# A transformer block on one core: the first norm moved to the token layout, and a new order of work on five engines

## The reference

```python
h = _layernorm(x) * (1 + ca) + sa                                # first norm
x = x + ga * _L0_attn_ref(h, Wqkv, bqkv, Wout, bout, rel_emb)    # 16 heads of 8, relative bias, softmax
h = _layernorm(x) * (1 + cb) + sb                                # second norm
x = x + gb * _L0_ffn_ref(h, ...)                                 # router, 16 experts, top 4
# second block, its own modulations
h = _layernorm(x) * (1 + ca) + sa                                # third norm
x = x + ga * _L1_attn_ref(h, Wk, Wv, Wo, gate, freqs)            # running sums of v * rotor, and of v * conj(k shifted)
h = _layernorm(x) * (1 + cb) + sb                                # fourth norm
x = x + gb * _L1_ffn_ref(h, W_r, W_k, W_v, mu_r, mu_k)           # mix with the token before, sigmoid, squared relu
```

## Time and profile before

| what | us |
|---|---|
| median of 3 runs | 1566.75 (1566.13 to 1572.26) |
| the profiled execution | 1568.34, its span 1566.6 |
| busy in the span: PE, DVE, ACT, POOL | 1409.5, 1180.5, 856.1, 304.8 |
| setup, to 47.7 | 47.7 |
| step 0, to 143 | 95.3 |
| a step of the loop | 90.5 |
| the last step, without an `a` | 65.6 |

### The profile page before, as it was taken

The page is one execution under the profiler, slowest core; times in us unless marked ns, Lnnn a source line. Parts: engine busy times, 40 slices in busy tenths (PEclk is TensorE's granted clock), DMA queues, the critical chain, the costliest instruction groups (busy, mean ns, idle before and its releaser), DMA issues.

```text
span 1566.6 us, 23671 instructions
## 1 busy us (share of the span) xinstructions
PE 1409.5 (90%) x7786; PEld 1076.5 (69%) x7786; DVE 1180.5 (75%) x2213; ACT 856.1 (55%) x1347; POOL 304.8 (19%) x261
## 2 busy tenths in 40 slices
PE   3678999999999999999999999999999998999976
PEld 2355776767677676767768676777767676786754
DVE  7535786878788687878968787887868788786865
ACT  1433756565474755646475565637556563756531
POOL 6012130312213030221303021130302112030210
PEclk7568998999999999999999999999999999999988
DMA  7012030301203030110303021030302003030000
GB/s 188 6 11 24 1 34 6 30 9 14 24 0 37 1 30 7 17 21 0 37 1 30 7 21 17 4 33 1 30 7 25 13 7 30 0 30 5 1 4 4
DMA packets 54664, 29.95 MB, mean 19 GB/s; under 512 B 3741, under 2 KB 53610, under 8 KB 54634
## 3 DMA queue, kind: packets, MB, share of 16 engines
q1 hardware_dynamic: 53968, 29.46, 15.8%
q10 hardware_dynamic: 666, 0.11, 0.1%
HBM read 8.20 MB, written 2.10 MB: 7 GB/s over the span
## 4 chain that ended last, share of the span: by engine, by line
PE 54%; DVE 14%; issue 13%; ACT 10%; DMA 3%; POOL 3%; SPq 1%; DVEq 0%; ACTq 0%; POOLq 0%
PE ring L642 11%; PE pb L734 7%; PE pa L656 7%; DVE smax L1440 4%; PE pb_v L686 3%; PE ring L563 3%; PE pb_v L698 2%; ACT prob L1041 2%; PE pa L576 2%; PE pb_v L705 2%; PE ring L629 2%; DMA q_rows<-m_sb 2%; DMA k_rows<-qk_part 2%; PE pb_k L671 2%; SPq L265 1%
## 5 line engine op out<-in xcount | busy, mean ns | idle before, releaser
L642 PE MATMUL ring<-ht,wgu 128*128 128x256 f32 x1024 | 241.6, 385 | 0.2 <-ACT sc_all L1084 0.2
L373 POOL TENSOR_TENSOR gsc<-gsc,sc_all 128x512 f32<-128x512 f32 x128 | 174.8, 1375 | 243.9 <-ACT gsc L1096 243.9
L642 PEld LDWEIGHTS ring<-ht,wgu 128*128 128x128 f32 x1024 | 193.8, 192 | 29.2 <-issue 3.2
L1091 ACT ACTIVATE gsc<-ring,gub_t 128x256 f32<-128x256 f32 x256 | 106.7, 467 | 143.1 <-DVE prob L1512 93.4
L734 PE MATMUL pb<-prod,wo 128*128 128x256 f32 x768 | 179.3, 383 | 2.9 <-DVE prod L1582 2.9
L734 PEld LDWEIGHTS pb<-prod,wo 128*128 128x128 f32 x768 | 144.9, 192 | 25.2 <-DVE prod L1582 6.6
L1440 DVE TENSOR_REDUCE smax<-ring 128x4 f32<-128x1024 f32 x128 | 154.1, 1219 | 8.7 <-PE ring L540 8.7
L1506 DVE TENSOR_SCALAR prob<-ring,gub_t 128x256 f32<-128x256 f32 x256 | 111.3, 475 | 62.0 <-PE ring L642 60.7
L1568 DVE TENSOR_TENSOR_SCAN prod<-keep,prod 128x512 f32<-128x512 f32 x128 | 154.0, 1213 | 0.6
L656 PE MATMUL pa<-prob,wdown 128*128 128x256 f32 x512 | 132.6, 388 | 0.1
L1041 ACT ACTIVATE prob<-ring 128x1024 f32<-128x1024 f32 x128 | 125.9, 1023 | 8.4 <-PE ring L563 6.7
(11 more groups left out here) (267 smaller groups left out, 2739.5 us busy)
## 6 DMA issues: line engine op xcount, KB each, us to landing
q_rows<-qk_part SPq DMA_DIRECT2D x144, 64.0 KB
k_rows<-qk_part SPq DMA_DIRECT2D x144, 64.0 KB
x_in<-in_L_attn_x_dram SPq DMA_DIRECT2D x16, 128.0 KB, 2.1
sc_all<-_L_ffn_gate_up_proj_dram SPq DMA_DIRECT2D x1, 2048.0 KB, 13.1
out_dram<-xo SPq DMA_DIRECT2D x16, 128.0 KB, 1.8
prob<-in_L_wmod_dram SPq DMA_DIRECT2D x2, 384.0 KB, 4.5
wo<-in_L_attn_Wo_dram SPq DMA_DIRECT2D x1, 512.0 KB, 4.3
wk<-in_L_attn_Wk_dram SPq DMA_DIRECT2D x1, 512.0 KB, 5.1
```

The costliest lines, as they stand in the source:

```text
L373: pool.tensor_tensor(gsc[:, n % NG, :], gsc[:, n % NG, :], sca, ALU.mult).then_inc(S["gsc"], 1)
L642: last = mm(ring[:, n % 2, g * 512 + j * L:g * 512 + (j + 1) * L], lhsT=wgu[:, 2 * n + j, g, :], rhs=ht[:, :], start=True, stop=True, skip ...
```

## The change

The first norm's statistics are taken on x_in as it is loaded, with the tokens on the partitions: VectorE takes them with BN_STATS and BN_AGGR over 128 features, and normalises there with one scalar per token (xn). TensorE then transposes both x_in and xn, and ScalarE modulates xn out of PSUM and copies xt. The products of mean, variance and broadcast of the first norm are gone. The 72 and 75 row products are the same as before. All engines' steps have a new order, and the setup's successor (`first`) and the last step (`last`) have lists of their own.

```diff
+            def stats(b):
+                need(dve, "x_in", b, 16)
+                for n in range(NT):
+                    nc.vector.bn_stats(st6[:, n, :], x_in[:, n, :]).then_inc(S["st1"], 1)
+            def moments(b):
+                for n in range(NT):
+                    nc.vector.bn_aggr(mv[:, n, :], st6[:, n, :]).then_inc(S["mv1"], 1)
+                need(dve, "mv1", b, NT)
+                ts(vepsh[:, :], mv[:, :, 1], EPS, None, ALU.add).then_inc(S["veps1"], 1)
+            def normal(b):
+                need(dve, "rstd1", b, 1)
+                need(dve, "xn_ps", b, 0)
+                for n in range(NT):
+                    ts(xn[:, n, :], x_in[:, n, :], mv[:, n, 0:1], rstdh[:, n:n + 1], ALU.subtract, ALU.mult).then_inc(S["xn1"], 1)
...
             def head_3(nx):
-                variance(nx, "1", hp, sqh)
-            def head_4(nx):
-                deviation(nx, "1", hp, rstdh)
+                need(pe, "xn1", nx, NT)
+                need(pe, "xt", nx, 1)
+                for n in range(NT):
+                    last = tr(hp[:, L + n * P:L + (n + 1) * P], xn[:, n, :], ident[:, :])
+                last.then_inc(S["xn_ps"], 1)
...
             def head_1(b):
-                need(act, "v_ps", b, 0)
-                square(b, "1", centh, sqh)
+                need(act, "xt_ps", b, 1)
+                need(act, "x1", b, 0)
+                af(xt[:, :], hp[:, 0:L], ACT.Copy).then_inc(S["xt"], 1)
             def head_2(b):
                 need(act, "mod_h", b, 1)
-                modulate(b, "1", centh, hta[:, :], mod_h, 0)
+                need(act, "v_ps", b, 0)
+                need(act, "xn_ps", b, 1)
+                af(hta[:, :], hp[:, L:2 * L], ACT.Identity, scale=mod_h[:, 1:2], bias=mod_h[:, 0:1]).then_inc(S["h1"], 1)
...
@@ SyncE, setup: ahead of the load of the expert weights @@
+            def spread_first():
+                sp.wait_ge(S["part2"], 1)
+                for a in range(3):
+                    for c in range(3):
+                        r = (a * 3 + c) * DH
+                        sp.dma_start(q_rows[r:r + DH, :, :], qk_part[:, a, 0, :]).then_inc(S["qk_rows"], 16)
...
@@ TensorE, step 0 @@
+            def first(a, nx):
+                turn_max(a)
+                turn_weights()
+                values_free()
+                scores_t(a, 0)
...
+                attn_out_2(a)
+                head_1(nx)
+                mean(a, "2", x1[:, :], "x1", pa, ())
+                head_3(nx)
+                variance(a, "2", pa, sq)
+                head_5(nx)
+                deviation(a, "2", pa, rstd)
+                router(a)
...
+                down_bias(a, nx)
+                turn_rotors(0)
+                turn_rotors(1)
+                down_pair(a, 0)
+                gate_up(a, 3)
...
@@ ScalarE, step 0 @@
+            def first(a, nx):
+                down_scaled()
+                copy_max(a)
+                exps(a, 0)
...
+                part_2(nx)
+                rotor_sines()
+                route(a)
+                copy_scores(a)
+                rotor_cosines()
+                copy_broadcast(a, 0)
...
@@ VectorE, step 0 @@
+            def first(a, nx):
+                maxima(a, 6)
+                maxima(a, 7)
+                split_max(a)
+                weights()
+                angles_2()
...
+                experts_out(a)
+                memory_weights()
+                maxima(nx, 0)
...
-def run(eng, head, step):
+def run(eng, head, first, step, last):
     head(0)
-    step(0, None, 1)
+    first(0, 1)
     step(1, 0, 2)
     with eng.Fori(2, B - 1) as i:
         step(i, i - 1, i + 1)
     step(B - 1, B - 2, None)
-    step(None, B - 1, None)
+    last(B - 1)
```

More of the change, by code:

```diff
@@ L304, in step, with last @@
                     store(b)
-            run(sp, head, step)
+            def first(a, nx):
+                load_x(nx)
+                spread_max(a)
+                spread(nx)
+            def last(b):
+                store(b)
+            run(sp, head, first, step, last)
             sp.wait_ge(S["out"], 16 * B)
@@ L966, in _ @@
+            run(pe, head, first, step, last)
         @block.scalar
@@ L1792, in run @@
+            run(dve, head, first, step, last)
+def run(eng, head, first, step, last):
     head(0)
-    step(0, None, 1)
+    first(0, 1)
     step(1, 0, 2)
```

689 lines of the change are left out of this document (454 added, 235 removed).

## The result

The changed kernel takes 1505.89 us (median of 4 runs, 1503.72 to 1511.7) against 1569.51 us before in the same comparison: ratio 0.960, 95% interval 0.956 to 0.9641. That is 4.0% faster. The forecast was 1540 us (1519 to 1566), so the time fell outside the range, on the fast side. The profiled execution took 1508.05 us, its span 1506.3.

The account below looks back on a forecast made before the run. VectorE's maxima were taken to bound each step's tail, TensorE the other 70.7 us. First step -6.9, fourteen steady steps -16.1 and end -4.4 made -27.4 from 1566.75: 1540 us, range 1519 to 1566.

Parts of the forecast that it names:

- the waits of the long half: TensorE's waits between first 75-row product and last gate and up product, 2.0 of 32.7 us; no gain counted.
- the rival "more": Steady steps: those waits go too and the tail overlaps better, 1.2 us more a step, 1523 us; chance 0.17.
- the other 70.7 us belong to TensorE ... so TensorE's work saved outside the tail counts in full: Steady step outside the tail: TensorE busy 30.68 of 32.70 and 24.93 of 25.30 us, so saved products shorten the step.
- The norm's -0.9: Steady step: first norm's mean, variance and broadcast products go (1.22 us), two transposes of xn come (0.3 us).
- -1.3: Steady step: fourth norm's broadcast (0.44) and second group of phase products (0.87) move into the tail, where TensorE would wait.
- The tail: From last gate and up product to first 75-row product, bound by VectorE's maxima: 19.8 us growing by 1.1 to 20.9.
- T0 of step 0: Setup: first 75-row product may start, the maxima sent to q_rows; at 57 us instead of 62.04, a gain of 5.
- the +6.3 from there to the experts: First step: ScalarE's rotor sines (2.9) and cosines (2.4) on the path, and head products ahead of the second broadcast (1.0).
- Rotors between the experts, 8 x 0.45: +3.6: First step: the eight rotor transposes placed among the expert products cost 3.6 us there.
- the transposes' -4.6: First step: the eight rotor transposes leave the attention stretch, saving 4.6 us.
- The slower rival: Steady steps: TensorE's low clock reaches 6.6 us past T0, costing 3.3 us a step, 1587 us; chance 0.15.
- The sum with the drain of 1.38 us: First step: a skill page's drain at each of three ScalarE table switches would make the gain 4 us less.

Follow-up runs that it names:

- e3: The kernel before with only the new first norm, in the old order: 1546.67 us (ratio 0.9845), a step 89.29 us.
- e8: e5 with the first group of time values done twice, unneeded, in the place the phase products left: 1539.51 us (0.9805), steps of 87.28 us.
- e6: The changed kernel with the old order on three engines from first 75-row product to first gate and up product, steady steps only: 1568.73 us (1.001).
- e1: The changed kernel with five gate and up pairs ahead of the first down product in the first step: 1491.55 us (0.9489).
- e10: e2 with added TensorE products that nobody needs, in the setup and around batch 0's score products: 1480.75 us (0.9434).
- e12: e2 with unneeded TensorE products in the setup, between attention and experts, in the first step's tail and in the last step: 1477.78 us (0.941).
- e2: e1 with the scaling of wo and wk moved into VectorE's wait for the first gate and up products: 1483.09 us (0.9453).
- e9: The kernel before with three unneeded fp32 products over 128 rows added in each tail: 1567.53 us (0.9995), steps of 90.4 us.
- e5: The changed kernel with the second group of phase products back behind the first 75-row product: 1552.55 us (0.9879), steps 88.3 us in the mean.
- e7: e2 with GpSimd's memset and weight copies and ScalarE's wdown scaling later in setup, and rotors, maxima and experts mixed finer: 1485.13 us (0.9468).

## Why the prediction was wrong, step by step

Two steps of the sum failed above all. In the steady step it took off only the products that go or move, and put the waits of the long half at nothing. In the first step it gave the new order of the experts the price of its transposes alone. Even the rival "more", 1523 us, lies 17 us above the result: the time is the sum of a steady gain of 72.9 us where 16.1 were forecast, and a loss of 19.6 at the start where a gain of 6.9 was.

**The steady step: -1.1 forecast, -5.2 measured.** The failed step is "the other 70.7 us belong to TensorE ... so TensorE's work saved outside the tail counts in full", taken as if only that counted. The norm's -0.9 was -1.24 (e3). The fourth norm's broadcast and the phases were put at -1.3, but the place of the phases alone is worth 1.95 (e8), because what follows them, the tables and the products that wait for them, moves up with them (the new waits in e8's rows). The waits of the long half I had in hand as the rival "more" (2.0 us of 32.7) and gave it 0.17: they went, from 2.4 us (70.71 less 68.30) to 0.56, and with them their first-product surcharge. Together this is 3.9 us of order (steps of 85.33 against 89.29 in e3), all of which disappears with the old middle (e6). I had compared the lists by what is moved and not by who waits for whom in the new list. The tail was forecast at 20.9 and is 20.35: VectorE is busy 17.43 us in it, 1.8 more than before where I added 1.1 by the earlier trace rows, and 0.55 of that shows; the rest went into its waits.

**BN_STATS** (no price, taken at 0.2 each): 0.24, from timeline of DVE in the setup, with the normalisation of the same kernel:

```profile
4.01 0.49 DVE L1619 BATCH_NORM_STATS2 st<-x_in 128x6 f32<-128x128 f32 x2 [2.39 <-DMA x_in<-in_L_attn_x_dram]
...
6.66 3.68 DVE L1631 TENSOR_SCALAR xn<-x_in,mv,rstdh 128x128 f32<-128x128 f32 x2 [0.91 <-POOL rstdh L367]
```

**Setup and first step: -6.9 forecast, +19.6 measured.** T0 of step 0 is right: 57 forecast, 57.43 measured; so are the wait for o_tok (5.30 in the earlier trace rows, 0.97 now) and the +6.3 from there to the experts (+6.7). Three things failed. The step "Rotors between the experts, 8 x 0.45: +3.6" priced the transposes and not the order they came with: the experts took 45.0 us, forecast 28.2. That is 16.8 us, shown by e1, and the lists show that the lag shrank from five pairs to three. Second, the attention stretch lost 3.8 us and not 9.4, since TensorE stayed at 1.2 GHz: +5.5, which e10 shows by taking 6.3 out. Before, the clock rose in the midst of the rotor transposes, after three groups of them back to back (timeline of PE, kernel before):

```profile
70.56 1.02 PE L456 MATMUL pb_v<-ident,cos_r 128*128 128x128 f32 x4
71.42 0.60 PE L456 MATMUL pb<-ident,cos_r 128*128 128x128 f32 x4
```

The 75-row products behind them took 0.60 us and not 1.03. So the transposes' -4.6 priced work and not what it did for the clock; that they brought it up is read from the order of events, no run here takes them away alone. Third, the tail of the step took 22.7 and not 19.4, its mean clock 0.62; e12's filling gets 1.0 us of that back, and what holds the rest is open. (The prediction's own terms for this tail add up to 19.2, so to 147.3 and not 147.5.)

**The end: -4.4 forecast, -7.0 measured**: 4.6 in step 15 and 2.4 from its h3 on. The rearranged gaps gave less, step 15's middle more, as in the steady steps. No experiment took this apart, but e2 has the same lists here and is 2.6 us shorter from T0 of step 15 on, with the last step's phases and output products at full clock; so a part of what the gaps failed to give went to low clock.

**The clock.** That the low clock of the old tail is hidden was right (e9). The slower rival, "if low clock reaches past T0", did not occur here but is real: e5 shows it at 1.0 us a step on average, where 3.3 was estimated. Its point "against", that products run almost without a pause before T0, is by e5 and e8 the one that decides: one group of products more or less turns it. The Trainium skill, "TensorE: Matmul & The Clock Gate", section "HAM oscillation — how this bites in real kernels", warns of pauses inside a loop that bring the clock down in each turn; e5 agrees, with a fall of the clock in each of its steps and, in the rows above, a pause of 2.23 us.

**The table loads.** The sum with the drain of 1.38 us in the Trainium skill, "ScalarE: Activation LUTs", section "What ACT_TABLE_LOAD costs", is not borne out: the load starts as the activation ahead of it ends, takes 1.28 us, and the sine follows at once (timeline of ACT, changed kernel).

```profile
89.14 0.63 ACT L1167 ACTIVATE qk_part<-qk 128x512 bf16<-128x512 f32 x1 [0.77 <-POOL qk L373]
89.78 1.28 ACT L1124 ACT_TABLE_LOAD   x1
91.08 1.91 ACT L1124 ACTIVATE sin_r<-prod 128x2048 f32<-128x2048 f32 x1
```

## What to carry to other kernels

When a new list of instructions is priced, add up for each wait the chain behind it in the new list: how many independent pieces are in flight between a product and the one that consumes its result. Here five pairs against three was 16.5 us in one step, and waits of 0.2 to 0.8 us, each too small to name, with the slower first products behind them, made most of a gain of 4% (3.9 us of order in each of 14 steps, of 63.6 us in all). A low clock costs only where TensorE sets the end, so look at who ends the wait next to it; where it does, work that nobody needs is a cheap probe, and sometimes a gain. And compare two runs by their marks before crediting an edit with their difference: of the 8.5 us between e1 and e2, 4.2 were the edit's.

## What the hardware showed that I had not expected

- Some VectorE operations stand still beside a GpSimd memset or copy: the two normalisations took 3.68 us beside a memset of 3.50 us, and 0.60 without it (e7). With the memset later, a copy of 128x2 took 3.39. Others don't: the two BN_STATS took 0.49 beside the memset of q_rows and 0.46 to 0.48 later. The cast of the maxima took 1.91 beside a copy of the expert weights and 0.18 elsewhere.
- The granted clock in the records is 1.00 from 0 to 106 us in the changed kernel, while eight 75-row products of batch 0 took 1.86 to 1.89 us and not 1.04. In e2 it is the same (1.86 us, and no record of the clock before 87.9 us). Until its first change in these traces this column can't be relied on; the durations of equal products can.
- Doubling five 72-row groups kept the clock up in the old tail in one step of 14; three products over 128 rows in fp32 did in 7 of 14, with less than their time added to the step (1.3 us of products, the step 0.1 shorter). They also stand in other places, so rows, type and place are not told apart.
